# The experts' up products of a decoder layer: fp32 matmuls, or three fp32r passes over weights parted on chip

## What is computed

```python
xn = _rms_norm(x, scale)
ids = jnp.argmin(_dist2(xn, centroids), axis=-1)
for e in range(N_EXPERTS):
    h = jnp.einsum('bsd,dh->bsh', xn, up_w[e])
    a, g = jnp.split(h, 2, axis=-1)
    y = jnp.einsum('bsh,hd->bsd', a * jax.nn.silu(g), down_w[e])
    out = jnp.where((ids == e)[..., None], y, out)
return out + skip
```

## Time and profile before

| | |
|---|---|
| Median of three runs | 1350.71 us (1348.08 to 1352.39) |
| Profiled execution | 1350.49 us, span 1348.8 us |
| TensorE matmuls, busy | 1223.9 us, 91% |
| VectorE, ScalarE, GpSimd busy | 811.2, 611.4, 413.7 us |
| HBM traffic | 84 GB/s over the span |

### The profile page before, as it was taken

The page is one execution under the profiler, slowest core; times in us unless marked ns, Lnnn a source line. Parts: engine busy times, 40 slices in busy tenths (PEclk is TensorE's granted clock), DMA queues, the critical chain, the costliest instruction groups (busy, mean ns, idle before and its releaser), DMA issues.

```text
span 1348.8 us, 29314 instructions
## 1 busy us (share of the span) xinstructions
PE 1223.9 (91%) x9542; PEld 915.5 (68%) x9543; DVE 811.2 (60%) x2110; ACT 611.4 (45%) x1288; POOL 413.7 (31%) x712
## 2 busy tenths in 40 slices
PE   6497999999999999999999999999985289999997
PEld 4274778778787877878787787878765145555554
DVE  3737667777786877778687777877644611211211
ACT  3426456464746646474654647465442122222211
POOL 1310324233142423314142331414122234444352
PEclk9598999999999999999999999999998589999998
DMA  8402520303213030321303032130383012121121
GB/s 265 126 1 110 222 107 17 111 16 109 80 52 117 16 109 16 109 80 48 121 16 109 16 109 77 48 124 9 111 324 113 16 49 64 51 62 53 55 66 28
DMA packets 51768, 112.29 MB, mean 83 GB/s; under 512 B 7333, under 2 KB 38863, under 8 KB 44944
## 3 DMA queue, kind: packets, MB, share of 16 engines
q1 hardware_dynamic: 45456, 96.81, 21.3%
q0 software_dynamic: 5616, 14.43, 3.6%
q10 hardware_dynamic: 656, 0.52, 0.1%
HBM read 89.72 MB, written 22.94 MB: 84 GB/s over the span
## 4 chain that ended last, share of the span: by engine, by line
PE 76%; DVE 10%; ACT 6%; issue 5%; DMA 2%; POOL 1%; SPq 0%; DVEq 0%; ACTq 0%; POOLq 0%
PE bank L1505 69%; PE bank L1540 3%; DVE a_p L1295 2%; PE bank L1706 2%; ACT shared L823 2%; PE bank L1869 1%; DMA rows_skip<-shared 1%; ACT shared L878 1%; ACT a_p L818 1%; DVE b_ql L1199 1%; DVE a_split L1227 1%; DVE a_split L1226 1%; DVE a_split L1225 1%; DVE a_ss L1236 1%; ACT a_sq L741 1%
## 5 line engine op out<-in xcount | busy, mean ns | idle before, releaser
L1505 PE MATMUL bank<-shared 128*128 128x256 f32 (+4 forms) x1730 | 320.3, 376 | 27.6 <-POOL shared L1030 11.3
L1505 PEld LDWEIGHTS bank<-shared 128*128 128x128 f32 (+2 forms) x1730 | 219.8, 166 | 88.7 <-issue 31.7
L1295 DVE TENSOR_TENSOR a_p<-a_p,eb 128x385 f32<-128x385 f32 x256 | 125.9, 555 | 75.6 <-ACT a_p L818 75.6
L1505 PE MATMUL bank<-up,shared 128*128 x312 | 143.8, 604 | 11.1 <-issue 11.1
L991 POOL TENSOR_SCALAR a_rz<-a_ms 128x2 f32<-128x2 f32 x16 | 3.1, 191 | 407.5 <-ACT a_sq L842 407.5
L818 ACT ACTIVATE a_p<-bank 128x385 f32<-128x385 f32 x256 | 105.1, 504 | 44.3 <-PE bank L1505 44.2
L1482 DVE TENSOR_TENSOR shared<-bank,shared 128x512 f32<-128x512 f32 x39 | 27.0, 692 | 153.7 <-ACT shared L876 153.7
L1505 PEld LDWEIGHTS bank<-up,shared 128*128 128x128 f32 x312 | 56.9, 192 | 75.6 <-issue 75.6
L876 ACT ACTIVATE shared<-bank 128x512 f32<-128x512 f32 x39 | 23.3, 597 | 137.2 <-PE bank L1505 137.2
L1505 PE MATMUL bank<-down,shared 128*128 x312 | 76.8, 390 | 7.2 <-ACT shared L878 7.2
L823 ACT ACTIVATE shared<-bank 128x512 f32<-128x512 f32 x128 | 66.1, 603 | 35.3 <-PE bank L1505 35.3
(11 more groups left out here) (237 smaller groups left out, 2724.8 us busy)
## 6 DMA issues: line engine op xcount, KB each, us to landing
w_low<-low_w SPq DMA_DIRECT2D x44, 1024.0 KB, 4.8
up<-in_L_ffn_up_w SPq DMA_DIRECT2D x8, 1024.0 KB, 13.9
x_in<-in_x SPq DMA_DIRECT2D x16, 256.0 KB, 2.7
shared<-in_ctx SPq DMA_DIRECT2D x16, 256.0 KB, 3.1
rows_x<-shared SPq DMA_DIRECT2D x16, 256.0 KB, 5.8
rows_skip<-shared SPq DMA_DIRECT2D x16, 256.0 KB, 6.2
down<-in_L_ffn_down_w SPq DMA_DIRECT2D x8, 512.0 KB, 12.3
toep<-a_hT SPq DMA_DIRECT2D x1, 3072.0 KB, 10.2
```

What stands on the lines that cost most here:

```text
L1295: tt(a_p[:, n_ % NPA], a_p[:, n_ % NPA], eb[:, n_], ALU.mult).then_inc(sig["a_p"], 1)
L1505: return mm(out, lhsT=lhsT, rhs=rhs, start=first, stop=last, **kw)
```

## The change

The up products become three passes over fp32r parts. The weights' parts `up_hi` and `up_low` are made on chip: ScalarE rounds (`round_up_weights`), VectorE subtracts (`rest_of_up`), in turn 18 and behind the routing. `up_hi` lies over buffers of the turns that are dead by then, for which the buffers in `shared` are carved in another order. The parts of a tile's rows are made in the expert stage: ScalarE's copy writes `m_xhi`, VectorE's `rest_of_rows` makes `m_xlow`. The unused `r_pp` goes, and in turn 19 the squares for the lengths are written to `b_f`, not `b_zT`. The core of the diff, without the carving:

```diff
             for e in range(E):
-                sp.dma_start(up[:, e], w_view(d["L0_ffn_up_w"][e])).then_inc(s_wmoe, 16)
+                sp.dma_start(up[:, e], w_view(d["L0_ffn_up_w"][e])).then_inc(s_up[e], 16)
                 sp.dma_start(down[:, e], w_view(d["L0_ffn_down_w"][e])).then_inc(s_wmoe, 16)
...
+        def round_up_weights(which):
+            for e in which:
+                act.wait_ge(s_up[e], 16)
+                copy(flat(up_hi[:, e]), flat(up[:, e])).then_inc(s_up_hi, 1)
...
             if Dd:
                 copy(flat(d_qT_hi[:]), full(act, it, "D.q")[:]).then_inc(sig["d_qhi"], 1)
+            if it.first == B + 2:
+                after(act, "x1_kept", B - 1)
+                round_up_weights(range(3))
...
+            if it.first == B + 2:
+                after(act, "c_nx", c)
+                round_up_weights(range(3, E - 1))
+                taken(act, it, "D.out")
+                round_up_weights(range(E - 1, E))
...
         def transposed(k, u):
             after_tile(act, "m_x", k, u)
-            copy(m_xT[:, u].rearrange("p c s -> p (c s)"), bank[u][:, 0:C * P]).then_inc(mig[u]["m_xT"], 1)
+            copy(flat(m_xhi[:, u]), bank[u][:, 0:C * P]).then_inc(mig[u]["m_xT"], 1)
...
+        def rest_of_up(halves):
+            for n in halves:
+                e, c_ = n // C, n % C
+                if c_ == 0:
+                    dve.wait_ge(s_up_hi, e + 1)
+                ins = tt(up_low[:, e, c_], up[:, e, c_], up_hi[:, e, c_].bitcast(F32), ALU.subtract)
+            ins.then_inc(s_up_low, len(halves) // C)
...
+            if it.first == B + 2:
+                rest_of_up(range(0, 8))
             if Dd:
                 ps = full(dve, it, "D.out")
...
                 stats(c_x2, c_st, c_mv2, "c_stats2", "c_mv2", dd)
+            if it.first == B + 2:
+                rest_of_up(range(8, 12))
...
+        rest_of_up(range(12, 16))
+        def rest_of_rows(k, u):
+            after_tile(dve, "m_xT", k, u)
+            tt(flat(m_xlow[:, u]), bank[u][:, 0:C * P], flat(m_xhi[:, u]).bitcast(F32), ALU.subtract
+               ).then_inc(mig[u]["m_xl"], 1)
...
                 tt(m_out[:, u], bank[DOWN_BANK[u]][:, 0:D], m_skip[:, u], ALU.add).then_inc(mig[u]["m_out"], 1)
+                if u == 0:
+                    for v in range(nxt):
+                        rest_of_rows(k + 1, v)
...
-        pe.wait_ge(s_wmoe, 16 * 2 * E)
+        pe.wait_ge(s_wmoe, 16 * E)
+        pe.wait_ge(s_up_low, E)
...
-            def up_half(u, half):
-                for c in range(C):
-                    w = up[:, bass.ds(expert[u], 1), c, half * EH:(half + 1) * EH]
-                    ins = product(bank[2 + 2 * u + half][:], m_xT[:, u, c], w.rearrange("p o n -> p (o n)"),
-                                  c == 0, c == C - 1)
+            def up_half(u, half, x_low_new):
+                for x, w_part in ((m_xhi, up_hi), (m_xhi, up_low), (m_xlow, up_hi)):
+                    if x is m_xlow and x_low_new:
+                        after_tile(pe, "m_xl", k, u)
+                    for c in range(C):
+                        w = w_part[:, bass.ds(expert[u], 1), c, half * EH:(half + 1) * EH]
+                        ins = product(bank[2 + 2 * u + half][:], x[:, u, c], w.rearrange("p o n -> p (o n)"),
+                                      c == 0 and x is m_xhi and w_part is up_hi, c == C - 1 and x is m_xlow)
                 return ins
```

More of the change, by code:

```diff
@@ L243, in _build @@
     s_fold = sem("bias_through_hidden_weights")
+    under_phase1 = ExitStack()
+    up_hi = sbuf(under_phase1, "up_hi", [P, E, C, 2 * EH], F32R)
+    under_phase1.close()
     b_kh, b_kl, b_qh, b_ql = (sbuf(ctx, name, [P, C, S], F32R) for name in ("b_kh", "b_kl", "b_qh", "b_ql"))
@@ L251, in _build, with carver @@
     place = {}
-    def carver():
-        at = [0]
+    def carver(first=0):
+        at = [first]
         def carve(name, shape, dt=F32):
@@ L277, in _build @@
     w1o = p1("w1o", [P, C, D])
+    rec = p1("rec", [P, 3, S])
+    rec_few = p1("rec_few", [P, 16])
+    x1 = p1("x1", [P, T, D])
+    c_in = p1("c_in", [P, T, D])
+    b_ctxT = p1("b_ctxT", [P, C, S])
+    b_xl = p1("b_xl", [P, T, D])
+    b_xT = p1("b_xT", [P, C, S])
+    b_v = p1("b_v", [P, T, D])
+    b_nm = p1("b_nm", [P, T, C, 4, 32])
     w11 = p1("w11", [P, C, HID])
+    b_p = p1("b_p", [P, NPB, T, S])
+    b_zT = p1("b_zT", [P, C, S])
+    b_yT = p1("b_yT", [P, C, S])
+    b_hT = p1("b_hT", [P, J, S])
     w12 = p1("w12", [P, J, D])
@@ L287, in _build @@
     lam = p1("lam", [P, 3])
[L289 to L303, removed]
     b_q = p1("b_q", [P, T, D])
-    b_hT = p1("b_hT", [P, J, S])
     b_st = p1("b_st", [P, T, 6])
@@ L514, in each @@
                     body(Turn(phase, k))
-    s_route, s_pp, s_wmoe = map(sem, ("routing_chain", "prefixes_made", "experts_loaded"))
+    s_route, s_pp, s_wmoe = map(sem, ("routing_chain", "prefixes_made", "down_weights_loaded"))
+    s_up = [sem(f"up_weights_loaded{e}") for e in range(E)]
+    s_up_hi, s_up_low = sem("up_weights_rounded"), sem("up_weights_rest_made")
     pa.close()
@@ L531, in _build @@
     pr.close()
+    under_up = ExitStack()
+    up_low = sbuf(under_up, "up_low", [P, E, C, 2 * EH], F32R)
+    under_up.close()
     up = sbuf(ctx, "up", [P, E, C, 2 * EH])
     down = sbuf(ctx, "down", [P, E, EJ, D])
[L534 to L543, removed]
+    m_xhi = sbuf(ctx, "m_xhi", [P, 2, C, P], F32R)
+    m_xlow = sbuf(ctx, "m_xlow", [P, 2, C, P], F32R)
+    UP_HI_END = E * C * 2 * EH - 5 * C * S
+    p3 = carver(UP_HI_END)
+    r_id = p3("r_id", [P, 4, TILES_MAX])
+    moe = carver(UP_HI_END + 160)
+    m_row = moe("m_row", [P, 2, 2, 1], U32)
+    m_token = moe("m_token", [P, 2, 1], U32)
+    m_in = moe("m_in", [P, 2, D])
+    m_skip = moe("m_skip", [P, 2, D])
+    m_sg = moe("m_sg", [P, 2, EH])
+    m_h = moe("m_h", [P, 2, EH])
+    m_hT = moe("m_hT", [P, 2, EJ, P])
+    m_out = moe("m_out", [P, 2, D])
     oh = p3("oh", [P, NT, E])
-    r_pp = p3("r_pp", [P, NT, E])
     r_tot = p3("r_tot", [P, NT, E])
@@ L560, in _build @@
     number = p3("number", [P, NT, 2, TILES_MAX], F16)
-    r_id = p3("r_id", [P, 4, TILES_MAX])
     io_p = p3("io_p", [P, 1])
@@ L572, in _build @@
     s_iota, s_numbered = sem("iotas_made"), sem("one_hot_numbered")
-    BY_TILE = {"m_loaded": 16, "m_skip": 16, "m_row": 1, "m_x": 1, "m_xT": 1, "m_up": 1, "m_silu": 1,
+    BY_TILE = {"m_loaded": 16, "m_skip": 16, "m_row": 1, "m_x": 1, "m_xT": 1, "m_xl": 1, "m_up": 1, "m_silu": 1,
                "m_h": 1, "m_ht": 1, "m_hT": 1, "m_down": 1, "m_out": 1, "m_stored": 16}
@@ L809, in turn @@
                     for t in range(T):
-                        nc.scalar.activation(b_zT[:, t], c_rows[:, t, 0:D], ACT.Square,
+                        junk = b_f if it.first == B + 3 else b_zT
+                        nc.scalar.activation(junk[:, t], c_rows[:, t, 0:D], ACT.Square,
                                              accum_out=c_nx[:, t:t + 1]).then_inc(sig["c_nx"], 1)
@@ L1474, in _ @@
         assert link[0] == ROUTE_ALL
+        rest_of_up(range(12, 16))
[3 more added lines that the diff above has]
+               ).then_inc(mig[u]["m_xl"], 1)
+        for u in range(2):
+            rest_of_rows(0, u)
         def of_tile(which, i):
@@ L1837, in _ @@
         pe.wait_ge(s_route, ROUTE_ALL)
-        pe.wait_ge(s_wmoe, 16 * 2 * E)
+        pe.wait_ge(s_wmoe, 16 * E)
+        pe.wait_ge(s_up_low, E)
         def transpose_in(k, u):
             after_tile(pe, "m_loaded", k, u)
-            after_tile(pe, "m_xT", k, u, 0)
+            after_tile(pe, "m_xl", k, u, 0)
             for c in range(C):
@@ L1885, in step @@
             after_tile(pe, "m_hT", k, 1, 0)
-            up_half(0, 0)
-            up_half(0, 1).then_inc(mig[0]["m_up"], 1)
+            up_half(0, 0, True)
+            up_half(0, 1, False).then_inc(mig[0]["m_up"], 1)
             if n == 2:
@@ L1891, in step @@
                 after_tile(pe, "m_out", k, 1, 0)
-                up_half(1, 1)
+                up_half(1, 1, True)
             turn_hidden(0)
             if n == 2:
-                up_half(1, 0).then_inc(mig[1]["m_up"], 1)
+                up_half(1, 0, False).then_inc(mig[1]["m_up"], 1)
             down_tile(0)
```

## The result

The change made the kernel slower by a third of a percent: 1354.53 us (median of 20 runs, 1351.47 to 1359.95) beside 1350.15 us for the kernel before (20 runs, 1346.02 to 1354.46). The ratio is 1.0034, with a 95% interval of 1.0023 to 1.0046. The forecast was 1335.2 us, with a range of 1330 to 1343.

What follows compares the result with a forecast made beforehand. TensorE's matmuls were taken to set the expert stage's pace. From 1350.5 us, 24.8 saved (1.26 in each of 19 pairs, 0.84 for the lone tile) and 9.5 added by the parting gave 1335.2 us, range 1330 to 1343.

Steps and rivals of the forecast that it cites:

- The parting: Splitting the up weights into rounded parts and rests, before the expert stage: 9.5 us more, from (a), (b) and (c).
- (a): Eight VectorE rests ahead of the sum out of bank `D.out`, which they delay: cost 4.9 us.
- (b): Four VectorE rests beside GpSimd's norms, one small GpSimd instruction getting in behind each rest: cost 3.1 us.
- (c): Four VectorE rests behind the routing, each of two GpSimd gathers waiting for the rest in progress: cost 1.5 us.
- The matmul's price, 0.216: Expert stage: an fp32r matmul with 512 moving columns taken at 0.216 us, between bounds of 0.2145 and 0.236.
- The chain beside `up_half(1, 1)`: Silu, product and turning of tile 0 take 1.72 us; the half shrinks to 1.30, TensorE waits 0.42, gain 0.
- the first step of the table: From a pair's start to the turning of tile 0's hidden rows: 5.25 us before, 4.41 forecast.
- the gain of 0.42 in `up_half(1, 0)`: The half behind tile 0's turning gains 0.42 us a pair, the turned rows' copy being ready by about 1185.3.
- four signs of being wrong: Matmuls 0.23 us or more apart; no idle before tile 0's turning; `D.out` sum near 1041.4; gathers over 3 us later.
- Rival 5: Expert stage: what is saved is waited for elsewhere in the pair, leaving only the 9.5 us cost: 1360.0 us, chance 0.02.
- Rival 3: Expert stage: an fp32r matmul costs 0.236 us, so the gain is 17.7 us in all: 1342.3 us, chance 0.08.
- Rivals 1, 2 and 4: Rests and GpSimd don't meet: 1331.9, chance 0.22; GpSimd gets nothing in between: 1339.4, 0.15; matmul costs 0.429: 1426.9, 0.04.

Runs made afterwards that it cites:

- the run with the gather later: Changed kernel, with GpSimd's gather of tile 1's skip rows waiting until TensorE has turned tile 0's hidden rows: 1337.83 us.
- the late read: TensorE reads tile 1's expert behind tile 0's matmuls: 1323.74 us on the changed kernel with gather behind turning and rests spread; 1337.26 on the kernel before.

## Why the prediction was wrong

- **The parting, 9.5 us: right.** (a) 4.9 forecast, 4.8 measured. (b) 3.1 forecast, 2.9 measured: one small GpSimd instruction gets in behind each rest, as taken. The Trainium skill (SBUF — State Buffer, section Who interferes with whom) states that a `tensor_tensor` with both inputs in SBUF contends with GpSimd's reads; the trace agrees, with 1.10 and 1.06 us for steps that take 0.22 and 0.20 alone. (c) 1.5 forecast, 1.6 measured, by a middle way that no row stood for: the first two gathers took 2.08 and 1.67 us beside the rests, 0.83 and 0.71 more than in the kernel before (1.25 and 0.96). The Trainium skill's inference in the same section, that making descriptors needs an interface which a `tensor_tensor` leaves free, gave the prediction 0.4 for (c), and that did not come. The gather also reads its row numbers (`sorted_row`) from SBUF, so the trace doesn't tell whether that read or the writing of descriptors was held. The roundings on ScalarE cost nothing, as forecast: none stands ahead of anything that was waited for.
- **The matmul's price, 0.216: too low.** It measured 0.227. The forecast put the weight load as the limit at 256 columns and gone at 512, and took almost the lower bound. The difference of 0.011 lies on 18 matmuls of a pair, 0.2 us; over the stage about 4 us of the 24.8. Why it is 0.227, no run shows.
- **The chain beside `up_half(1, 1)`: right that it sets the pace, but read too long.** TensorE waits ahead of the turning, 0.22 us in place of 0.42: the cover is 6 x 0.227 = 1.36, and the chain, from 1191.01 to 1192.59, is 1.58. The prediction read it as 1.72, as long as its cover, with nothing to spare. But in rows 3 VectorE's product ends 0.20 us ahead of the turning, in the changed kernel 0.06: the chain had 0.14 us to spare. That the first step of the table is met within 0.02 us is luck: tile 0's two halves took 2.85 us (1188.16 to 1191.01) where the forecast makes them 2.69, and the chain was 0.14 shorter.
- **The step that failed is the gain of 0.42 in `up_half(1, 0)`.** It rested on the sentence that the copy of the turned rows is ready ahead of the shorter half's end, and that took the turning's signal to arrive as promptly as it had in the kernel before, 0.04 us. It came 1.4 us later. `down` then waits for the copy, and of 20.6 us that the stage can give at 0.227 a matmul, 16.9 are lost. None of the prediction's four signs of being wrong looked at that copy. That the late signal takes the gain is shown by the run with the gather later; why the signal is late stays open.
- **Rival 5 came closest,** at a chance of 0.02. It said that the saving would be waited for elsewhere in the pair, and named GpSimd's queue; it was dismissed because GpSimd is not half busy in the stage. Its busy share did not change (93.14 us of the stretch before, 92.87 after). What did is where one of its transfers stood in the pair, and that counted together with something else of the changed kernel, since the kernel before bears the same place. The change moved TensorE's turning from behind GpSimd's gather (issued from 1183.01 to 1183.98 us in the pair of rows 3, the turning at 1184.03) to beside it (1192.43 to 1193.40 and 1192.59).
- **Rival 3** took 0.236 for a matmul; 0.227 lies half way between it and the forecast. **Rivals 1, 2 and 4** didn't happen: rests and GpSimd do meet, GpSimd gets in between, and a register-addressed fp32r matmul costs 0.227, not 0.429.

## What to carry to other kernels

A stage that is shortened on one engine moves that engine's work against every other queue. Before counting a saving, lay the new times of the signals over the transfers of the queues that were "not busy", and check by moving one of them what the pair then takes. Work that is added to an engine was cheapest here in the gaps that the trace names with their releasers: 16 rests cost 9.3 us in three blocks, and 6.6 of it came back when they were spread. An edit found on the way (here the late read) is to be tried on the kernel before as well.

## What the hardware showed that was not expected

TensorE's signal came long after the recorded end of the work. (The profile's ends of matmuls are modelled, so the trace doesn't show whether the last result was late or only its signal.) ScalarE's start and the recorded update of the semaphore agree that the turning's signal came up to 1.8 us after its last transpose, while the matmuls behind it started on time, 0.227 us apart. In the pair shown the signal of `up_half(1, 0)`, whose last matmul started 1.26 us behind the last transpose, came 0.08 us after that of the turning. In the whole program of the changed kernel no other signal of TensorE that the trace recorded was late by over 0.15 us, but for that of `up_half(1, 0)` in the eighteenth pair (0.5 us), which came 0.1 us after the turning's.

What has to come together is known only in part. Needed in all runs that showed it was an indirect transfer that GpSimd had started some 0.1 to 1.4 us before the turning's last transpose; it was never seen without one, and moving gather and store away cleared it in 20 of 20. Not needed are fp32r matmuls behind the turning, the wait behind it, or direct neighbourhood. What TensorE reads around it matters: 17 of 20 late with the rests' tile, 3 of 20 with the rounded weights, at the same times of GpSimd. And the kernel before never showed it, neither with its gather moved to that place nor with gather and store both there. Never taken out were the fp32r matmuls ahead of the turning (`up_half(1, 1)`), which every run with a late signal had. Nor is the turning's signal the only one: in the version with the late read, the eighteenth pair has that of `up_half(1, 0)` 0.76 us late, with a gather started 0.18 us ahead of its last matmul; in the run with the gather later, that place leaves the same signal on time in 17 pairs. Why, stays open.
